# An adaLN mix and quantised feed-forward kernel: row gathers ahead of the large gather, blocks of tiles 2 and 3 placed together

## The reference

```
W   = weights[condition]                         # 64 x 32 x 32
y   = einsum('bct,bcd->bdt', x, W)               # the mix
xf  = y.reshape(-1, 512).astype(bfloat16)
qg, sg = dynamic_quant(xf, inv_gate)             # xs = xf * inv; scale = max|xs| / 127; round
qu, su = dynamic_quant(xf, inv_up)
gate = qg @ w_gate.T * sg * s_wgate              # 512 -> 256
up   = qu @ w_up.T   * su * s_wup
inter = clip(silu(gate) * up, -10, 10).astype(bfloat16)
qi, si = dynamic_quant(inter, inv_inter)
out  = x + qi @ w_down.T * si * s_wdown          # 256 -> 512
```

## Time and profile before

| | |
|---|---|
| median of 3 runs | 94.34 us (94.31 to 94.59) |
| the profiled execution's own time | 93.95 us |
| its span, first to last instruction | 92.1 us |
| mean granted TensorE clock | 0.98 |
| busy, us (share of the span) | TensorE 71.7 (78%), VectorE 70.7 (77%), ScalarE 63.5 (69%), GpSimd 64.1 (70%) |

### The profile page before, as it was taken

The page is one execution under the profiler, slowest core; times in us unless marked ns, Lnnn a source line. Parts: engine busy times, 40 slices in busy tenths (PEclk is TensorE's granted clock), DMA queues, the critical chain, the costliest instruction groups (busy, mean ns, idle before and its releaser), DMA issues.

```text
span 92.1 us, 1613 instructions
## 1 busy us (share of the span) xinstructions
PE 71.7 (78%) x479; PEld 45.1 (49%) x486; DVE 70.7 (77%) x144; ACT 63.5 (69%) x113; POOL 64.1 (70%) x76
## 2 busy tenths in 40 slices
PE   3940795623997378999999999999999886977560
PEld 3920354311785155565664656646566554633120
DVE  3600259999639978799999989989989998698830
ACT  4320358697487879989898898898988987731100
POOL 3677057162548799999999999999999966258200
PEclk9999999999669999999999999999999999999999
DMA  0999974470002030434607526113022020220353
GB/s 8 223 337 406 314 234 109 78 236 0 7 0 80 34 103 11 114 118 117 221 23 219 144 87 227 62 53 121 0 114 81 33 114 4 109 114 7 119 223 121
DMA packets 7225, 10.88 MB, mean 118 GB/s; under 512 B 2544, under 2 KB 2608, under 8 KB 7216
## 3 DMA queue, kind: packets, MB, share of 16 engines
q1 hardware_dynamic: 6864, 10.43, 35.1%
q0 software_dynamic: 208, 0.33, 1.3%
q10 hardware_dynamic: 144, 0.01, 0.1%
HBM read 6.31 MB, written 4.46 MB: 117 GB/s over the span
## 4 chain that ended last, share of the span: by engine, by line
POOL 31%; issue 27%; PE 11%; ACT 10%; DVE 9%; DMA 9%; POOLq 1%; DVEq 0%
POOL xs L204 13%; POOL qm L227 7%; DMA rows<-mix_w,row 7%; POOL clipped L211 7%; POOL xm L220 5%; PE y_ps L579 5%; PE gu_ps L601 3%; ACT q L276 2%; DMA tokens<-token 2%; ACT y_bf L269 2%; PE y_ps L638 2%; ACT q_t L283 2%; PE qt_ps L585 1%; DVE w_t L451 1%; ACT w_t L300 1%
## 5 line engine op out<-in xcount | busy, mean ns | idle before, releaser
L204 POOL TENSOR_TENSOR xs<-y_bf,inv_in 128x1024 f32<-128x1024 bf16 x15 | 32.1, 2143 | 6.5 <-ACT y_bf L269 6.2
L579 PE MATMUL y_ps<-x_sb,mix_all 128*128 128x512 f32 x32 | 19.0, 677 | 12.1 <-ACT mix_all L335 7.3
L276 ACT ACTIVATE q<-xs,rscale 128x512 f32<-128x512 f32 x32 | 21.3, 712 | 1.3 <-DVE rscale L418 1.0
L283 ACT ACTIVATE q_t<-qt_ps 128x1024 bf16<-128x1024 f16 x16 | 16.4, 1024 | 6.3 <-PE qt_ps L585 6.2
L400 DVE TENSOR_REDUCE y_ps<-xs 128x2 f32<-128x1024 f32 x15 | 18.3, 1220 | 0.0
L638 PE MATMUL o_ps<-w_t,qm_t 128*128 128x512 bf16 x72 | 17.7, 379 | 0.8 <-ACT qm_t L295 0.5
L601 PE MATMUL gu_ps<-raw,q_t 128*128 128x256 bf16 x128 | 17.6, 280 | 0.0
L601 PEld LDWEIGHTS gu_ps<-raw,q_t 128*128 128x128 bf16 x128 | 12.3, 97 | 9.3 <-issue 7.4
L579 PEld LDWEIGHTS y_ps<-x_sb,mix_all 128*128 128x128 f32 x32 | 5.2, 206 | 13.6 <-issue 13.0
L424 DVE TENSOR_TENSOR gu<-gu_ps,s_in 128x512 f32<-128x512 f32 x16 | 10.9, 683 | 1.2 <-PE gu_ps L601 1.2
L220 POOL TENSOR_TENSOR xm<-clipped,inv_mid 128x256 f32<-128x256 bf16 x16 | 10.8, 675 | 1.4
(11 more groups left out here) (58 smaller groups left out, 71.6 us busy)
## 6 DMA issues: line engine op xcount, KB each, us to landing
x_sb<-x SPq DMA_DIRECT2D x16, 256.0 KB, 2.9
out<-res SPq DMA_DIRECT2D x16, 256.0 KB, 2.0
raw<-w_gate SPq DMA_DIRECT2D x1, 512.0 KB, 4.9
raw<-w_up SPq DMA_DIRECT2D x1, 512.0 KB, 6.2
raw<-w_down SPq DMA_DIRECT2D x1, 512.0 KB, 8.8
picked_dram<-picked SPq DMA_DIRECT2D x1, 256.0 KB, 2.9
mix_all<-picked_dram SPq DMA_DIRECT2D x4, 48.0 KB, 2.1
rows<-mix_w,row POOLq DMA_INDIRECT x4, 6.1
```

The costliest lines, as they stand in the source:

```text
L204: nc.gpsimd.tensor_tensor(xs[t % N][:, :, :], y_bf[t % N][:, :].unsqueeze(1).to_broadcast([P, 2, T]), inv_in[:, :, :], ALU.mult).then_inc( ...
L276: nc.scalar.activation(q[t % N][:, m, :], xs[t % N][:, m, :], ACT.Copy, bias=ROUND_TO_F16, scale=rscale[:, t, m:m + 1]).then_inc(q_done, 1)
L283: nc.scalar.activation(q_t[t % N][:, :, :, :], qt_ps[t % 2][:, :, :, :], ACT.Copy, bias=-float(OFFSET)).then_inc(qt_out, 1)
L579: nc.tensor.matmul(y_ps[t % 2][:, :], mix_all[:, t, :], x_sb[:, t * T:(t + 1) * T], start=True, stop=True).then_inc(y_done, 1)
```

## The change

GpSimd issues the four row gathers one behind the other and the large gather after them. The blocks of tiles 2 and 3 are no longer placed by two engines in steps 1 and 2 of their loops: a new function `place_pair` on ScalarE waits for both gathers and copies, in four instructions, for each of the four places on the diagonal the blocks of both tiles at once, in step 1 behind the eviction of `inv_mid` and ahead of the quantisation of tile 0. TensorE waits for it ahead of the mix of tile 2, and for no placement ahead of tile 3's. TensorE also gets fourteen more `keep_warm` products behind the first `spread`s. Transfers of `x` and of the weights are issued as before.

```diff
             pool.wait_ge(row_done, 1)
-            gather_rows(0)
-            gather_rows(1)
+            for t in range(EARLY):
+                gather_rows(t)
             pool.indirect_dma_start(picked[:, :], None, mix_w.rearrange("s c d -> s (c d)"),
...
-            for t in range(2, EARLY):
-                gather_rows(t)
...
+            def place_pair():
+
+                for t in range(2, EARLY):
+                    act.wait_ge(rows_in[t], 16)
+                for j in range(PER):
+                    nc.scalar.activation(mix_all[j * C:(j + 1) * C, 2:EARLY, j * C:(j + 1) * C],
+                                         rows[j * C:(j + 1) * C, 2:EARLY, :], ACT.Copy).then_inc(placed_pair, 1)
...
                     spread_to_sbuf(3, inv_mid[:, :], inv_mid_ps[:, 0:I])
+                    place_pair()
...
                 if i in (1, 2):
-                    place_lower(i + 1)
                     for c in range(IC):
                         part_of_down(i - 1, c)
...
-                if i in (1, 2):
-                    place_upper(i + 1)
                 if i in (1, 2, 3):
                     for c in range(IC):
                         fold(i - 1, c)
...
-                if t < EARLY:
+                if t < 2:
                     pe.wait_ge(placed_upper, PER // 2 * (t + 1))
                     pe.wait_ge(placed_lower, PER // 2 * (t + 1))
+                elif t == 2:
+                    pe.wait_ge(placed_pair, PER)
...
             spread(2 * TC, 2 * IC, s_in_ps)
+            keep_warm(WARM_UP, y_ps[1])
             pe.wait_ge(spread_evicted, 2)
```

More of the change, by code:

```diff
@@ L119, in adaln_ffn @@
         channel_done, in_row_done, row_done = sem("channel_done"), sem("in_row_done"), sem("row_done")
-        placed_upper, placed_lower = sem("placed_upper"), sem("placed_lower")
+        placed_upper, placed_lower, placed_pair = sem("placed_upper"), sem("placed_lower"), sem("placed_pair")
         spread_done, spread_evicted = sem("spread_done"), sem("spread_evicted")
```

## The result

The changed kernel takes 90.6 us in the median (89.99 to 91.9, four runs) against 94.47 for the kernel before (94.31 to 95.39, four runs); the ratio is 0.955, with a 95% interval of 0.945 to 0.965. In a second measurement it gave 91.1 against 95.69, ratio 0.957 (0.949 to 0.966). The forecast was 91.0, with a range of 89.7 to 92.6. The profiled execution took 90.21 us, with a span of 88.4 instead of 92.1.

A forecast was written before the change was run, and what follows sets the result against it. GpSimd and VectorE pace the middle, engines waiting for each other the fill; 3.36 us saved there gives span 92.1 - 3.36 = 88.7, and from the median 94.34 - 3.36 = 91.0 us, range 89.7 to 92.6.

The forecast's parts named there:

- The waits that go: In the fill, ScalarE's waits of 0.80 and 1.52 us and smaller ones vanish; tile 0's Silu comes 3.36 us sooner.
- ScalarE as the pace: From the four copies to tile 0's Silu, ScalarE's queue alone sets the pace: 8.74 us without a wait.
- the two removals: VectorE's held-up copies of tiles 2 and 3 (4.11 us) go, and TensorE's 3.24 us wait for tile 3's blocks shrinks.
- Gathers: GpSimd's large gather, issued 2.47 us later, lands at 14.2 (13.4 to 15.1); the later blocks stay hidden at tile 4's mix.
- Warm-up products: Fourteen more on TensorE before tile 0's blocks delay nothing; gain at the first mix 0 to 0.95 us, taken as 0.
- The warm-start rival: TensorE's clock is up for the first two mixes, 4.8 us gained in all: 89.5 us, chance 0.13.
- Folds held up by GpSimd: VectorE's folds wait for GpSimd's products, 1.1 us lost: 92.1 us; chance 0.16 together with dearer copies or a clock fall.
- blocks too late: TensorE's mix of tile 4 waits for blocks after the later large gather: 95.7 us at 13 us latency, chance 0.06.

The follow-up runs named there:

- the repetition: The changed kernel run once more with no edit, on the chip of the first experiments: 91.1 us (90.62 to 92.68).
- one with an earlier start: Changed kernel with SP waiting for tile 1's rows before issuing the weights (down weights first) and x of tiles 2 to 5: 92.17 us (88.78 to 93.77).
- large gather third: Changed kernel with the gathers in their old order, the large one after the row gathers of tiles 0 and 1: 91.58 us (89.56 to 91.93).

## Why the prediction was right

*The waits that go.* Right. The fold came at 15.18, 0.69 us long, the mix of tile 3 at 18.25 (18.2 forecast), the Silu at 22.98 (23.29), GpSimd's product of tile 4 at 25.71 (25.6). The span came out at 88.4 for 88.7. The agreement of the product is partly luck: the Silu came 0.3 sooner than forecast, but the product starts 2.73 behind it instead of 2.30, since GpSimd's own work, from the product of tile 3 at 22.30 on, leaves it no gap there any more. And the gain of 3.36 us was sized for one measurement: it came out at 3.9 between the medians there and at 4.6 in the second one, where the kernel before took 95.69 (mean granted clocks 0.92 to 0.98, for 0.98 in the profile before). No trace shows the kernel before in that measurement, so where the further 1.2 us over the forecast gain lie is not known.

*ScalarE as the pace.* Right, and shown: four more copies delayed the Silu by all of their 1.05 us. The four copies took 1.09, for 1.08 taken and 0.96 to 1.5 as bounds. The chain from the copies to the Silu took 8.25 for 8.74: two weight parts and the eviction behind them 1.43 and not 1.57, the eviction of q 0.90 and not 1.04. The rows that I had taken these distances from start each instruction behind the end of the one before (25.61 and 1.02 give 26.63, the next starts at 26.65); after the change neighbours overlap by about 0.1 us (18.52 and 1.03 give 19.55, the next starts at 19.42). Why they did not before is not shown. The chain started 0.18 later (14.73 for 14.55): the first rows landed 0.4 later, at 9.5 for 9.1, and the second mix gave 0.3 of that back, 1.38 long for 1.68.

*Which of the two removals made it.* The prediction put them side by side; the experiments part them. Without copies on VectorE but with tile 3's blocks late, nothing is gained (Silu at 28.47, 26.65 before). With early blocks but the copies on VectorE the Silu is at 24.73, 1.92 sooner than before; with the copies on ScalarE, in the repetition, it is at 23.57, another 1.16 sooner. So the blocks' early place is the larger part, and VectorE's held-up copies the smaller.

*Gathers.* Right: the large one landed at 14.5 (14.2 forecast, 13.4 to 15.1), and its place made no difference. *Warm-up products.* Taken at nothing, and nothing was measured. The warm-start rival did not come true: the clock was up before the first mix, with the added products and without them, and at half again when it ran, behind 3.33 us in which TensorE had nothing to do. With 56 products, which left 1.89 us empty, the first mix did run at full clock. *Folds held up by GpSimd* fell, *blocks too late* fell for this kernel and came true in one with an earlier start.

What the prediction did not see: TensorE's gap ahead of tile 5, 2.26 us for 1.87 before, after which the clock fell in some executions. Of the seven profiles that keep this part of the kernel it fell in four, at 29.0 to 29.9 us (56 products, large gather third, four copies more, copies on VectorE); there GpSimd's step from tile 5 to 6 took 4.86 to 5.36 us, in the other three 3.97. With the gap bridged the times of 91.9 and 92.68 did not come again. And the 6 us of the row gathers, which I took as given, were mostly the doing of the weights and x beside them.

## What to carry to other kernels

In the fill of a pipeline, lay out the queue of the engine that will be left without a wait, add its distances from start to start, and check every input against that list; a step moved ahead of its need can be worth more than the engine time it saves. When a start gets faster, look at once for the transfers and the clock that the old delay had covered. Small gathers that open the critical path should not share the DMA engines with bulk loads that nobody needs yet; but putting the loads off gave nothing here until what they then held up, the blocks first of all, was looked after as well.

## What the runs showed of the hardware

- A 128-row gather of 128 bytes a row lands 2.4 us after issue (median of four) with the weight loads and four x loads put off, and 6.5 us beside them.
- A VectorE copy from SBUF to SBUF that starts beside a GpSimd product ends with it (the first of four 2.05 us, beside a product of 2.14, the other three about 0.19 each), while an elementwise product of PSUM and SBUF operands keeps its 0.69 us.
- The clock's level at the first mixes differs between executions of one kernel (half from 9.7 to 13.1 or from 9.3 to 16.1) and moves the fill by some 0.5 us (13.46 or 13.99 from the first rows' landing to the Silu).
- Behind a gap of 2.26 us in TensorE's work the clock fell in four of seven profiles and stayed at full in three.
- Four ScalarE copies of 32 x 64 take 1.09 us. The formula of the Trainium skill (ScalarE: Activation LUTs, What ACT_TABLE_LOAD costs) gives, as an estimate, some 240 ns for each, near the trace's 0.27 from start to start, but the overlap of neighbours that it states did not appear in these small copies. Between the larger instructions behind them it did (0.57 us long, 0.47 from start to start).
